# Attention values turned round: v as the weights of four column tiles, one batch of matmuls a row, and the sums inverted and spread by matmul

## What is computed

```python
x = roll(groupnorm(x), (-3, -3))                     # 32 groups of 4 channels
x = windows(x)                                       # 8 x 8 windows of 7 x 7 = 49 tokens, 128 channels
q, k, v = split_heads(x @ qkv_weight.T + qkv_bias)   # 8 heads of 16
attn = softmax(q * 16 ** -0.5 @ k.T + rel_pos_bias + mask)   # 49 x 49 for each window and head
x = (attn @ v) @ proj_weight.T + proj_bias
x = image + unroll(x)
out = x + conv3x3(groupnorm(x), kernel)
```

## Time and profile before

| | us |
|---|---|
| median of three runs | 3633.04 (3629.91 to 3636.04) |
| the profiled execution | 3628.35 |
| its span, first to last instruction | 3626.5 |
| granted TensorE clock over the span | 0.995 |

### The profile page before, as it was taken

How to read it: one execution, slowest core, us unless ns; L and a number is a source line. 1 busy time by engine, 2 the same in 40 slices (tenths; PEclk the granted TensorE clock), 3 DMA queues, 4 the chain that set the end, 5 groups by cost and what they waited for, 6 DMA issues and landing times.

```text
span 3626.5 us, 141183 instructions
## 1 busy us (share of the span) xinstructions
PE 3415.0 (94%) x57227; PEld 2799.3 (77%) x57227; DVE 3045.9 (84%) x7552; ACT 2630.5 (73%) x5857; POOL 2322.2 (64%) x3674
## 2 busy tenths in 40 slices
PE   2999999999999999999999999999999999999997
PEld 1778778778778778778777778777778778788785
DVE  5788888888888888888888888888888888888885
ACT  1777777777777777777777777777777777777772
POOL 4476666766666766666766666766667766657763
PEclk9999999999999999999999999999999999999998
DMA  2011101111101111101111111111111111111001
GB/s 57 20 30 33 33 25 30 36 33 36 33 25 30 36 33 36 33 23 33 35 34 35 28 28 33 33 35 36 28 28 33 33 36 33 30 25 33 18 18 29
DMA packets 213331, 113.75 MB, mean 31 GB/s; under 512 B 8784, under 2 KB 212688, under 8 KB 212688
## 3 DMA queue, kind: packets, MB, share of 16 engines
q1 hardware_dynamic: 212688, 104.72, 11.0%
HBM read 53.31 MB, written 51.38 MB: 29 GB/s over the span
## 4 chain that ended last, share of the span: by engine, by line
PE 51%; DVE 23%; POOL 12%; issue 11%; ACT 2%; SPq 0%; DVEq 0%; POOLq 0%; DMA 0%; ACTq 0%
PE conv_ps L994 14%; PE qkv_ps L875 10%; PE attn_ps L913 7%; PE probsT_ps L899 7%; PE scores_ps L888 5%; DVE s_sb L743 4%; POOL s_sb L404 3%; DVE plane_lo L755 3%; PE misc_ps L875 2%; DVE s_max L748 2%; DVE x_b L791 2%; PE misc_ps L961 2%; PE misc_ps L957 2%; PE misc_ps L951 2%; POOL x_n L444 1%
## 5 line engine op out<-in xcount | busy, mean ns | idle before, releaser
L404 POOL TENSOR_TENSOR s_sb<-s_sb,s_max 113x392 f32<-113x392 f32 x1024 | 1027.7, 1004 | 1127.6 <-DVE s_max L748 1123.2
L899 PE MATMUL probsT_ps<-ident,probs 113*128 113x113 f32 x4096 | 586.4, 265 | 72.6 <-ACT probsT L466 72.5
L460 ACT ACTIVATE probs<-s_sb 113x392 f32<-113x392 f32 x1024 | 551.6, 539 | 128.3 <-POOL s_sb L404 124.8
L432 POOL TENSOR_TENSOR plane<-x_n 128x224 f32<-128x224 f32 x896 | 601.3, 692 | 18.7
L913 PEld LDWEIGHTS attn_ps<-v,probsT 128*49 128x49 f32 x16384 | 465.4, 125 | 181.9 <-issue 160.3
L748 DVE TENSOR_REDUCE s_max<-s_sb 113x8 f32<-113x392 f32 x1024 | 574.6, 561 | 35.3
L527 ACT COPY v<-qkv_ps 64x256 f32<-64x256 f32 (+2 forms) x1280 | 393.6, 327 | 287.7 <-PE qkv_ps L875 281.6
L466 ACT COPY probsT<-probsT_ps 128x392 f32<-128x392 f32 x1024 | 489.5, 478 | 144.6 <-PE probsT_ps L899 140.4
L743 DVE TENSOR_TENSOR s_sb<-scores_ps,bias 113x392 f32<-113x392 f32 x1024 | 564.7, 551 | 8.1 <-PE scores_ps L888 8.1
L913 PE MATMUL attn_ps<-v,probsT 128*49 128x34 f32 x16384 | 566.5, 214 | 3.5 <-DVE o_sb L719 0.6
L899 PEld LDWEIGHTS probsT_ps<-ident,probs 113*128 113x128 f32 x4096 | 431.4, 141 | 129.3 <-ACT probs L460 86.0
(11 more groups left out here) (142 smaller groups left out, 6706.9 us busy)
## 6 DMA issues: line engine op xcount, KB each, us to landing
x_in<-in_x_dram SPq DMA_DIRECT2D x224, 224.0 KB, 2.8
out_dram<-x_out SPq DMA_DIRECT2D x224, 224.0 KB, 2.5
x_b<-in_L_conv_w_dram SPq DMA_DIRECT2D x1, 576.0 KB
x_b<-L_conv_pruning_mask_dram SPq DMA_DIRECT2D x1, 576.0 KB
x_n<-_conv_rel_pos_table_dram SPq DMA_DIRECT2D x14, 10.7 KB
x_n<-in_mask_dram SPq DMA_DIRECT2D x1, 196.0 KB
w_in<-n_L_conv_qkv_weight_dram SPq DMA_DIRECT2D x1, 192.0 KB
ident<-in_ident_dram SPq DMA_DIRECT2D x1, 64.0 KB
```

The costliest lines, as they stand in the source:

```text
L404: nc.gpsimd.tensor_tensor(s, s, top, ALU.subtract).then_inc(sub_ready, 1)
L432: last = nc.gpsimd.tensor_tensor(plane[:, t % 2, j], *sums[j])
L460: nc.scalar.activation(probs[0:QP, slot % 2, :, :, 0:N], s_sb[0:QP, slot % 4], ACT.Exp)\
L899: last = nc.tensor.transpose(probsT_ps[:, w * 128:w * 128 + QP], probs[0:QP, u % 2, w].rearrange("p e m -> p (e m)"), ident[0:QP, 0:QP])
```

## The change

- `values(row)` runs once a row, in unit 2 (mod 4) (`VALUES_AT = 6`), instead of once a unit. v is now the weight (32 columns: two heads of 16), the turned probabilities (49 columns) move. The pair of heads picks one of four column tiles of 32, so the result has channels on its partitions: 8 windows x 4 pairs = 32 matmuls into `attn_ps[:, 0:392]`.
- 32 more matmuls have `head_ones` as weights (a 128 x 32 pattern of ones for each window) and add up, over the eight windows, the sums of the probabilities of every window and head in `attn_ps[:, 392:441]`: a window and head has a partition of its own.
- DVE inverts these sums, 128 x 49, in one instruction in unit 3 (mod 4). The job "rec" takes the place of "ot": eight f32 matmuls with 128 x 128 weights `head_rows[:, w]` spread the reciprocals of a window to the channels.
- ACT copies the values to `values_sb` (a new copy); DVE multiplies them by the spread reciprocals into `o_sb`, in one product of 392 columns. The four products, the two reciprocals of 16 columns and the transposes go.
- ACT casts `o_sb` to `oT_hi`; the low half is formed by POOL at the head of unit 1 (mod 4) of the next row, and "proj" waits for it.
- `probsT` has six slots. `x_out` has two slots instead of seven. `w_in` and `w_f` lie in `plane`, which is free during setup. POOL builds `head_ones` and `head_rows` in setup, 5 fills and 8 copies. v loses its columns of ones.

```diff
-LAG_T, LAG_PV = 2, 3
+LAG_T = 2
+PT_SLOTS = 6
+VALUES_AT = 6
+OUT_SLOTS = 2
...
-        for first, kind in ((OT_AT, "ot"), (PROJ_AT, "proj")):
+        for first, kind in ((OT_AT, "rec"), (PROJ_AT, "proj")):
...
+def row_of(i, u, first):
+    r, rest = divmod(u - first, PAIRS)
+    turn, r = divmod(r, ROWS)
+    return (i + turn) * ROWS + r if rest == 0 and live(i, turn) else None
...
             pool.wait_ge(const_in, 16 * N_CONST)
...
+            nc.gpsimd.memset(head_ones[:], 0.0).then_inc(head_consts, 1)
+            pool.wait_ge(head_consts, 1)
+            for e in range(2):
+                for a in range(2):
+                    diagonal = flat(head_ones)[ODD * e:ODD * e + ODD, a * HD + e::2 * HD + 2]
+                    nc.gpsimd.memset(diagonal, 1.0).then_inc(head_consts, 1)
+                    pool.wait_ge(head_consts, 2 + 2 * e + a)
+            rows = ident[:].rearrange("k (p x) -> k p x", x=2 * HD)
+            for w in range(NWIN):
+                last = nc.gpsimd.tensor_copy(
+                    head_rows[:, w, :].rearrange("k (p e d) -> k p e d", e=2, d=HD),
+                    rows[:, :, 2 * w:2 * w + 2].unsqueeze(3).to_broadcast((128, PAIRS, 2, HD)))
...
             def body(i):
                 for u in range(UNITS):
+                    row = row_of(i, u, VALUES_AT + 3)
+                    if row is not None:
+                        pool.wait_ge(oT_hi_ready, row + 1)
+                        nc.gpsimd.tensor_tensor(oT_lo[:].rearrange("p r (w c) -> p w r c", c=WIN),
+                                                o_sb[:].rearrange("p w (r c) -> p w r c", c=WIN),
+                                                oT_hi[:].rearrange("p r (w c) -> p w r c", c=WIN), ALU.subtract)\
+                            .then_inc(oT_lo_ready, 1)
                     if live(i):
                         pool.wait_ge(max_ready, i * UNITS + u + 1)
...
                     if live(i, 0 if u >= LAG_T else -1):
                         evacuate_probsT(i, i * UNITS + (u - LAG_T), u - LAG_T)
+                    row = row_of(i, u, VALUES_AT + 2)
+                    if row is not None:
+                        act.wait_ge(misc_free, rec_number(row) + 1)
+                        nc.scalar.copy(oT_hi[:].rearrange("p r (w c) -> p w r c", c=WIN),
+                                       o_sb[:].rearrange("p w (r c) -> p w r c", c=WIN)).then_inc(oT_hi_ready, 1)
                     misc(i, u, MID)
+                    row = row_of(i, u, VALUES_AT)
+                    if row is not None:
+                        act.wait_ge(attn_ready, row + 1)
+                        if row > 0:
+                            act.wait_ge(misc_free, rec_number(row - 1) + 1)
+                        nc.scalar.copy(values_sb[:], attn_ps[:, 0:RT].rearrange("p (w n) -> p w n", n=N))\
+                            .then_inc(values_copied, 1)
...
+                    row = row_of(i, u, VALUES_AT + 1)
+                    if row is not None:
+                        dve.wait_ge(attn_ready, row + 1)
+                        dve.wait_ge(values_copied, row + 1)
+                        vec.reciprocal(recip[:], attn_ps[:, RT:RT + N]).then_inc(recip_ready, 1)
...
-                        if kind == "ot":
+                        if kind == "rec":
...
+                            dve.wait_ge(misc_ready, misc_number(i + turn, kind, t) + 1)
+                            need(dve, oT_lo_ready, row)
+                            vec.tensor_tensor(o_sb[:], misc_ps[:, 0:RT].rearrange("p (w n) -> p w n", n=N),
+                                              values_sb[:], ALU.mult).then_inc(misc_free, 1)
...
-            def values(i, u):
...
-                for w in range(NWIN):
-                    p0, wp = ODD * (w % 2), w // 2
-                    at = (wp * 2 + pair % 2) * VW
-                    last = mm(attn_ps[p0:p0 + N, at:at + VW], probsT[:, u % 2, w, :], v[:, r % 2, w, pair, :],
-                              start=True, stop=True)
+            def values(row):
...
+                for w, pair in product(range(NWIN), range(PAIRS)):
+                    parts = slice(2 * HD * pair, 2 * HD * (pair + 1))
+                    mm(attn_ps[parts, w * N:(w + 1) * N], v[:, row % 2, w, pair, :],
+                       probsT[:, (row * PAIRS + pair) % PT_SLOTS, w, :], start=True, stop=True)
+                for w, pair in product(range(NWIN), range(PAIRS)):
+                    parts = slice(2 * HD * pair, 2 * HD * (pair + 1))
+                    last = mm(attn_ps[parts, RT:RT + N], head_ones[:, w, :],
+                              probsT[:, (row * PAIRS + pair) % PT_SLOTS, w, :],
+                              start=(w == 0), stop=(w == NWIN - 1))
                 last.then_inc(attn_ready, 1)
...
-                if kind == "ot":
-                    pe.wait_ge(attn_norm, (i * ROWS + (t + 1 if u >= OT_AT else t + 1 - ROWS)) * 2)
-                    for w in range(WP):
-                        last = nc.tensor.transpose(misc_ps[:, w * 128:w * 128 + QP], o_sb[0:QP, w, :], ident[0:QP, 0:QP])
+                if kind == "rec":
+                    pe.wait_ge(recip_ready, i * ROWS + (t + 1 if u >= OT_AT else t + 1 - ROWS))
+                    for w in range(NWIN):
+                        last = mm(misc_ps[:, w * N:(w + 1) * N], head_rows[:, w, :], recip[:], start=True, stop=True)
                 if kind == "proj":
+                    pe.wait_ge(oT_lo_ready, i * ROWS + (t + 1 if u >= PROJ_AT else t + 1 - ROWS))
```

More of the change, by code:

```diff
@@ L26 @@
 from contextlib import ExitStack
+from itertools import product
 import concourse.bass as bass
@@ L257, in build_block @@
         x_loaded = [sem(f"x_loaded{t}") for t in range(TILES)]
-        x_stored = [sem(f"x_stored{t}") for t in range(TILES)]
+        x_stored = [sem(f"x_stored{slot}") for slot in range(OUT_SLOTS)]
         misc_ready, misc_free = sem("misc_ready"), sem("misc_free")
@@ L296, in build_block @@
         wc_u = flat(x_b)[:, 0:PLANES * KW * C].rearrange("p (t c) -> p t c", c=C)
+        early = plane[:].rearrange("p s j r w -> p (s j r w)")
+        w_in, w_f = (early[:, j * 4 * C:(j + 1) * 4 * C].rearrange("p (t c) -> p t c", c=C) for j in range(2))
         wc_sum = flat(x_n)[:, 0:C]
@@ L574, in _ @@
             dve.sem_inc(rel_zeroed, 1)
-            for buf, value in ((v, 0.0), (probs, 0.0), (scores_ps, 0.0), (attn_ps, 1.0)):
+            for buf, value in ((v, 0.0), (probs, 0.0), (scores_ps, 0.0)):
                 vec.memset(buf[:], value)
@@ L579, in _ @@
             step(vec.memset(ones, 1.0))
-            for e in range(2):
-                step(vec.memset(v[ODD * e:ODD * e + N, :, :, :, 2 * HD + e:2 * HD + e + 1], 1.0))
             dve.wait_ge(const_in, 16 * N_CONST)
@@ L704, in body @@
                 for u in range(UNITS):
-                    n, rest = divmod(u - (LAG_PV + 2), 2)
-                    if rest == 0 and live(i, 0 if n >= 0 else -1):
-                        number, half = i * ROWS * 2 + n, n % 2
-                        dve.wait_ge(attn_ready, (number + 1) * 2)
-                        outputs = attn_ps[0:QP, 0:WP * 2 * VW].rearrange("p (a v) -> p a v", v=VW)
-                        vec.reciprocal(recip[0:QP, half], outputs[:, :, 2 * HD:VW]).then_inc(recip_ready, 1)
-                        dve.wait_ge(recip_ready, number + 1)
-                        if half == 0 and (not isinstance(number, int) or number > 0):
-                            turn = i if u >= 2 else i - 1
-                            dve.wait_ge(misc_ready, misc_number(turn, "ot", (n // 2 - 1) % ROWS) + 1)
-                        for pair in range(2):
-                            at = (half * 2 + pair) * 2 * HD
-                            last = vec.tensor_tensor(
-                                o_sb[0:QP, :, at:at + 2 * HD].rearrange("p w (e d) -> p w e d", d=HD),
-                                outputs.rearrange("p (w a) v -> p w a v", a=2)[:, :, pair, 0:2 * HD]
-                                .rearrange("p w (e d) -> p w e d", d=HD),
-                                recip[0:QP, half].rearrange("p (w a) e -> p w a e", a=2)[:, :, pair].unsqueeze(3)
-                                .to_broadcast((QP, WP, 2, HD)), ALU.mult)
-                        last.then_inc(attn_norm, 1)
```

79 lines of the change are left out of this document (37 added, 42 removed).

## The result

| | before | after |
|---|---|---|
| median of the runs taken together, us | 3631.47 | 4266.03 (4261.51 to 4267.98) |
| the profiled execution, us | 3628.35 | 4261.51 |
| its span, us | 3626.5 | 4259.7 |
| granted TensorE clock over the span | 0.995 | 0.952 |
| ratio after/before | | 1.1743 [1.1723, 1.1764] |

A forecast was written before the change was run, and what follows sets the result against it. The prediction took TensorE's stream to bound the kernel. The longer stream, +0.83 us a row over 256 rows (+213 us), and waits for POOL's low half (+220 us) on 3633 us gave about 4065 us, range 3830 to 4250.

The forecast's parts named there:

- What bounds the kernel: Whole kernel: TensorE's stream bounds it; a microsecond added there is a microsecond of time.
- Values and sums: TensorE's stream, added: 128 passes for values and sums, tiling changes included, 1.60 us a row.
- The round of four: Values and sums block: four passes, one on each column tile, all in flight, take 0.043 us.
- the 0.05 that would have said wrong: Sign for the values and sums block: the forecast is wrong if rounds of four take over 0.05 us.
- the rival of the shared path: Values and sums: the four column tiles share a path, rounds 0.06 to 0.087 us, 4190 to 4410 us; 11%.
- The 25 ns rule: Values and sums, rival: matmuls start 25 ns apart at the closest, 460 us more, 4530 us; 4%.
- rec: TensorE's stream, added: spreading the reciprocals in 16 f32 passes at 0.11 us, 1.88 us a row with its edges.
- the removed part: TensorE's stream: the old values blocks and the turn of the result go, 2.65 us a row.
- The wait for POOL's low half: proj in unit 1 (mod 4) waits for POOL, 3.6 + 2.0 + 1.5 us in each of 31 images, +220 us.
- DVE's microsecond: DVE has about 1 us less a row, which buys nothing since TensorE didn't wait for it.
- The clock: Rival: TensorE's clock falls in the new waits of 3 to 4 us, 45 us more, 4110 us; 10%.
- The range: Whole kernel: 3830 to 4250 us, holding the forecast, the first rival, the clock and part of the shared path.

The follow-up runs named there:

- low_dve: The changed kernel with the low half formed by DVE at the head of unit 1 (mod 4) instead of by POOL; 3875.15 us, 1.0673.
- rec_f16: The changed kernel with the reciprocals split into float16 halves and head_rows in float16, so rec is 16 float16 passes; 4154.9 us, 1.1438.
- fill_wait: The changed kernel with 115 and 85 unread float16 matmuls in units 9 and 25 ahead of proj's wait; 4143.28 us, 1.1408.
- before_order: The kernel before, plus one tiny POOL addition at the head of unit 1 (mod 4) for which proj waits; 3873.66 us, 1.0670.
- run 123: Not a label: part of "made the run 123 us faster", a time, said of fill_wait against the changed kernel; fill_wait measured 4143.28 us.
- before_norm_early: The kernel before with Newton ahead of the subtraction and the first group norm's jobs in units 20 and 21; 3627.01 us, 0.9982.
- serial_tiles: The changed kernel with the loops of values exchanged, so 16 passes in a row go to one column tile; one run, 5044.02 us.

## Why the forecast was wrong, point by point

- **What bounds the kernel** held: low_dve takes POOL's wait away and pays for the longer stream in full, 243 us.
- **Values and sums**, 1.60 us forecast, are 1.57 at the full clock (0.74 for the values, 0.83 for the sums with the way out), outside the stops. The round of four is 0.046 us against 0.043, under the 0.05 that would have said wrong. Loads of 32 columns take 123 ns, not 111, and it didn't matter. So the rival of the shared path is out.
- **The 25 ns rule** of the Trainium skill ("TensorE: Matmul & The Clock Gate", section "Wait — 56ns, not 53.3ns?") has a price of 1.8 us a row in the forecast, and the block shows none of it: 0.74 us for 64 passes is 11.5 ns a start. By this rule it would be 1.6 us, an estimate from the page's figure. In rec_f16, where all passes go through the whole array, the starts are 25 ns apart, so there the rule and the row agree. As I read these two rows, it holds where matmuls follow each other in one tile.
- **rec**, 1.88 us forecast, is 1.915; 191 ns for a load, 0.12 us from pass to pass. Together with the removed part the stream grew by 7.7 us an image (low_dve against before) and not by 6.6, 33 us in all. The three new blocks are 28.3 us an image where 3.48 x 8 = 27.8 were forecast; the larger part of the miss is what went: the removed blocks were 19.8 us an image, and the blocks around them became 0.9 shorter, 20.65 where 2.65 x 8 = 21.2 were forecast.
- **The wait for POOL's low half**: the mechanism held. Unit 9 has 4.0 us (forecast 4.3), unit 25 a median of 3.0 (3.2), units 13, 17, 21 and 29 have 1.0, 0.4, 0.6 and 0.3, 2.4 together (forecast 1.5). That is 9.2 us an image against 9.0, and 294 us in all against some 250, more often (191 times) than the 60 to 100 forecast, by the many short ones. That the whole idle time grew by 7.2 us an image, against +7.1, is in part luck. The wait swallowed 2.9 us of older ones, and not 1.9: the forecast overlooked the wait for probsT in unit 11, 1.2 us an image, which is half of the entry in the earlier trace rows. The stops without a releaser, 1.2 us an image, which it didn't have, made up for that.
- **DVE's microsecond** was worth nothing, as said: its share fell from 84% to 68%.
- **The clock** is the step that failed. The sum of the forecast has nothing for it; it stood as a rival at 10% and at 45 us: a wait in two, followed by 3 us at half speed, 1.5 us each. The runs show 5.0 us an image, 155 us in 31 images (4.7 an image by fill_wait, 4.6 in before_order). Both factors were too low. Nearly every long wait is followed by a slow stretch (65 spells in after, about two for each of 31 images, against 6 before), and a spell lasts 6.3 us (407.5/65) and not 3, so that it costs some 2.5 us. fill_wait, which keeps the array busy in the same waits, and before_order, which makes such waits in the kernel before, show it from both sides. The rows that I had, were of the end of the run; I took from them that the clock can fall, and no frequency. The kernel before has no waits of 3 us in its steady part. But its first images hold a case that would have given a price, a wait of 1.57 us that ends at 193.2, by windows:

```profile
190.00:193.90 3.90, 2.33 (x41) 2.10 (x36) 3.62 (x13) 3.04 (x7) 0.92 (x1) 1.00 0.02 4
193.90:200.70 6.80, 6.80 (x88) 5.27 (x86) 4.62 (x14) 2.41 (x7) 2.37 (x6) 0.50 0.00 0
```

A wait of half the length of the forecast's was followed by 6.8 us at half clock. With 3 us for each of the two long waits of every image the clock's term is 31 x 2 x 3 = 186 us (4251); even at the rival's 1.5 us it is 93 (4158), so it belonged into the sum.

- **The range**: 4250 was the end of the shared path's case. The clock and the forecast together were not put at its end, since the clock stood as a rival in place of the forecast. It was not one: it comes with the waits.

With the clock's term put right alone, the sum is 213 + 220 + 155 = 588 us, or 4221, inside the range; 635 were measured. The stream is 33 us above its term (7.7 x 32 = 246), the idle time 3 above (7.2 x 31 = 223), and some 11 us lie in the first and the last images. So it took the clock and the stream together to leave the range, by 16 us.

## What to carry to other kernels

Ask of each wait that a change gives to the bounding TensorE what the clock does behind it: in this kernel a wait of 3 to 4 us cost its length and about 2.5 us more, and filling it with useless matmuls made the run 123 us faster. Before an operation goes to an engine "with room", read that engine's list of work at the point where it is inserted: POOL was busy for 64%, and one instruction of 1 us there cost 391 us, since it stood behind 4 us of tiny steps and the rolls. And a shorter stream ahead of a wait for another engine buys only part of its length (rec_f16: 10.0 us of matmuls an image less, 3.3 us of time).

## What the runs showed of the hardware

- The clock fell to its lower level after waits of 3 to 4 us in a stream that is else 94% busy, after one of 1.57 us in before, and in before_norm_early after a stretch with 1.88 us of work in 3.00 and no wait over 1.12. In low_dve it stayed up after a stop of 1.9 us:

```profile
2144.00:2147.50 3.50, 2.90 (x143) 2.22 (x132) 2.04 (x6) 3.31 (x8) 3.50 (x7) 1.00 0.04 9
2147.50:2149.40 1.90, 0.02 (x4) 0.02 (x3) 0.76 (x2) 0.25 (x1) 1.65 (x3) 1.00 0.00 0
2149.40:2156.00 6.60, 6.60 (x109) 6.14 (x109) 4.30 (x10) 4.48 (x11) 2.70 (x3) 1.00 0.01 2
```

So the longest wait alone doesn't tell; what does was not settled.

- At the lower clock the distance from a matmul to the next is 1.8 times that at the full clock (1.79 over 295 us of after, 1.78 over 297 us of before_order), not 2.
- TensorE stops for 0.2 to 1.9 us within the block of sums without a releaser: 36 times and 27 us in after, 54 times and 45 us in low_dve, never in before. Fewer such stops follow in the qkv block behind it (14 times and 7 us in after). These kernels have 76683 matmuls in place of 57227, and the packets of the queue that brings instructions rise from 459 to 612 (7.52 to 10.03 MB). serial_tiles has the same 76683 and 612, but takes 4.74 us for the 128 passes in place of 1.57, and it has no such stop. So the stops come with the pace of the block and not with the number of instructions. That the instructions come too late for 128 short passes in 1.6 us fits this, but is not shown.
- Four f32 matmuls of 128 rows and 32 columns run at once in four column tiles if the order of the program alternates (11.5 ns a pass), and take about 37 ns a pass if 16 in a row go to the same tile.
